# A two-layer graph kernel: layer two's own-row factors kept on chip, and one statistics instruction for two blocks' last rows

## The reference

```python
h = maximum(layernorm(x), 0)
out = h @ W_self.T + b_self                       # layer one: mean over links
agg = segment_sum(h[dst] @ W_neigh.T + b_neigh, src); count = clip(links of a node, 1)
x = x + out + agg / count
h = maximum(layernorm(x), 0)
norm = deg**-0.5 [src] * deg**-0.5 [dst]          # layer two: symmetric norm
x = x + relu(segment_sum(h[src] * norm[:, None], dst))
```

## Time and profile before

| | |
|---|---|
| median of 3 runs | 1193.75 us (1192.7 to 1194.19) |
| profiled execution, its own time | 1191.59 us |
| its span (first to last instruction) | 1189.8 us |
| VectorE, ScalarE busy | 1045.1 us, 1033.9 us |
| TensorE, GpSimd busy | 851.3 us, 783.7 us |
| mean granted TensorE clock | 0.777 of full |

### The profile page before, as it was taken

One profiled execution on the slowest core, in us unless ns is written; L12 is line 12 of the kernel. 1 busy time (PEld: TensorE's weight loads), 2 busy tenths in 40 slices (PEclk: granted clock), 3 DMA queues, 4 the chain that ended last, 5 costly groups with the idle time before them and its releaser, 6 DMA issues.

```text
span 1189.8 us, 32033 instructions
## 1 busy us (share of the span) xinstructions
PE 851.3 (72%) x10194; PEld 772.0 (65%) x10292; DVE 1045.1 (88%) x2871; ACT 1033.9 (87%) x2679; POOL 783.7 (66%) x1034
## 2 busy tenths in 40 slices
PE   1488999999999999999999952444444444444444
PEld 1378999999999999999899952343343343334343
DVE  6889999999999999999988636888888888888886
ACT  1579999999999999999989926988888988889896
POOL 3735667766767767766656127777777777777771
PEclk6699999999999999999999985555555555555555
DMA  6326666666666766666655244888888888888884
GB/s 207 117 74 182 195 203 194 203 201 193 204 191 201 208 188 203 209 189 202 195 182 180 90 183 126 281 269 274 272 259 268 280 262 266 280 262 265 273 273 185
DMA packets 76797, 252.46 MB, mean 212 GB/s; under 512 B 16114, under 2 KB 16484, under 8 KB 76676
## 3 DMA queue, kind: packets, MB, share of 16 engines
q1 hardware_dynamic: 57412, 210.46, 54.8%
q0 software_dynamic: 19264, 40.48, 13.3%
HBM read 146.50 MB, written 104.37 MB: 211 GB/s over the span
## 4 chain that ended last, share of the span: by engine, by line
PE 32%; POOL 21%; issue 19%; ACT 16%; DVE 8%; POOLq 2%; DMA 1%; SPq 0%; ACTq 0%; DVEq 0%
POOL X L663 17%; ACT work L771 12%; PE p_O L958 11%; PE p_O L946 8%; PE p_T L901 5%; PE p_T L920 4%; DVE ST L1360 3%; ACT area L787 2%; POOL work L600 2%; PE p_T L864 1%; DVE area L1419 1%; POOL factor L636 1%; PE p_O L954 1%; ACT p_T L771 1%; ACT area L795 1%
## 5 line engine op out<-in xcount | busy, mean ns | idle before, releaser
L771 ACT ACTIVATE work<-X,shift,scale 128x128 f32<-128x128 f32 x1231 | 504.0, 486 | 1.8 <-DVE shift L1394 1.8
L1360 DVE BATCH_NORM_STATS2 ST<-X 128x6 f32<-128x256 f32 x1176 | 405.8, 415 | 14.3 <-DMA X<-x_table 7.0
L663 POOL DMA_INDIRECT X<-in_x,IDX x294 | 290.1, 987 | 101.2 <-issue 70.9
L663 POOL DMA_INDIRECT X<-x_table,IDX x294 | 285.6, 971 | 92.8 <-issue 89.9
L1000 PE MATMUL p_O<-work 32*128 32x128 f32 x1600 | 156.2, 436 | 150.2 <-ACT work L771 78.5
L1000 PEld LDWEIGHTS p_O<-work 32*128 32x128 f32 x1600 | 135.3, 323 | 164.2 <-issue 116.8
L1000 PE MATMUL p_T<-work 32*128 32x128 f32 x1536 | 150.0, 436 | 125.5 <-POOL work L604 70.2
L946 PE MATMUL p_O<-wnT,area 128*128 128x128 f32 x1568 | 216.9, 282 | 8.0 <-DVE area L1419 7.8
L1000 PEld LDWEIGHTS p_T<-work 32*128 32x128 f32 x1536 | 130.0, 323 | 138.4 <-issue 118.4
L958 PEld LDWEIGHTS p_O<-wsT,area 128*128 128x128 f32 x1568 | 206.0, 192 | 7.3
L958 PE MATMUL p_O<-wsT,area 128*128 128x128 f32 x1568 | 206.6, 275 | 5.1
(11 more groups left out here) (158 smaller groups left out, 913.8 us busy)
## 6 DMA issues: line engine op xcount, KB each, us to landing
x_table<-area SPq DMA_DIRECT2D x98, 528.0 KB
X<-x_table SPq DMA_DIRECT2D x98, 528.0 KB, 4.6
X<-in_x SPq DMA_DIRECT2D x98, 512.0 KB, 4.2
out_x<-area SPq DMA_DIRECT2D x98, 512.0 KB, 5.5
X<-in_x,IDX POOLq DMA_INDIRECT x294
X<-x_table,IDX POOLq DMA_INDIRECT x294
es<-in_src SPq DMA_DIRECT2D x1, 488.5 KB, 3.6
ed<-in_dst SPq DMA_DIRECT2D x1, 488.5 KB, 4.4
```

The costliest lines, as they stand in the source:

```text
L663: nc.gpsimd.indirect_dma_start(got(s)[:, k, 0:w], None, table, bass.IndirectOffsetOnAxis(ap=IDX[:, s, k:k + 1], axis=0)).then_inc(gathered ...
L771: last = nc.scalar.activation(o, row(l, s, r), ACT.Relu, bias=shift[:, s, r:r + 1], scale=scale[:, s, r:r + 1])
L1360: last = V.bn_stats(ST[:, s, r:r + 2, :].rearrange("p r k -> p (r k)"), of)
```

## The change

A new tensor F [128, 98, 11] holds the factors of all rows and all blocks. Layer one's reciprocal of the counts goes into F[:, i, 0:8] and stays there; `rc` and its wait for `dis_ready` are gone. ScalarE's copy of the link factors goes into F[:, :, 8:11] in place of `DISL`. In layer two GpSimd multiplies only F[:, :, 8:11], in place, by the gathered rows' column D; the product for the own rows is gone, and so are the waits for `x_loaded` and `scale_made`. `scales1` reads F at the block's index. From the third block of layer two on, the statistics of the 11th rows of an even block and the odd block behind it are taken by one instruction, which interleaves the two rows, in the odd block's step.

```diff
--- before.py
+++ after.py
@@ -257,7 +257,7 @@
         work = sb("work", [P, TB * EC])
         SRC = sb("SRC", [P, DRAWS, NB + max(LOT)], i32)
         DL = sb("DL", [P, PARTS, NB])
-        DISL = sb("DISL", [P, DRAWS, NB])
+        F = sb("F", [P, NB, ROWS])
         both = sb("both", [P, 2, NB])
 
         SLOT = ROWS * XW
@@ -272,7 +272,6 @@
         sd = sb("sd", [P, max(RING), ROWS])
         rstd = sb("rstd", [P, max(RING), ROWS])
         scale = sb("scale", [P, max(RING), ROWS])
-        factor = sb("factor", [P, max(RING), ROWS])
         shift = sb("shift", [P, max(RING), ROWS])
 
         KEPT = (ROWS, DRAWS)
@@ -300,7 +299,6 @@
         verdict = sb("verdict", [1, 4, CHECKS])
         bad = sb("bad", [1, 1])
         flag = sb("flag", [1, 1], i32)
-        rc = sb("rc", [P, HT, BT])
 
         def own(l, s):
 
@@ -623,28 +621,20 @@
 
                 i, s, _ = place(1, turn, off)
                 for k in range(n):
-                    _, q, uses = place(1, turn, off + k)
-                    pool.wait_ge(x_loaded[q], (uses + len(range(q, NB, RING[0]))) * 16)
-                    pool.sem_inc(idx_seen[1], 1)
+                    _, q, _ = place(1, turn, off + k)
                     pool.wait_ge(gathered[q], landed(1, q, turn, off + k))
                     pool.sem_inc(idx_seen[1], 1)
-                if not first(i, RING[1]):
-                    pool.wait_ge(scale_made, lots(turn, off) - RING[1] // 2)
+                if first(i, 1):
+                    pool.wait_ge(s_coded, 2 * TB)
                     pool.sem_inc(idx_seen[1], 1)
-                of_own = X[:, s:s + n, 0:BT * XW].rearrange("p n (j d) -> p n j d", j=BT)[:, :, :, D]
                 of_got = X[:, s:s + n, BT * XW:ROWS * XW].rearrange("p n (k d) -> p n k d", k=DRAWS)[:, :, :, D]
-                nc.gpsimd.tensor_tensor(factor[:, s:s + n, 0:BT], of_own, of_own, ALU.mult)
-                nc.gpsimd.tensor_tensor(factor[:, s:s + n, BT:ROWS], of_got,
-                                        DISL[:, :, bass.ds(i, n)].rearrange("p k b -> p b k"), ALU.mult
+                nc.gpsimd.tensor_tensor(F[:, bass.ds(i, n), BT:ROWS], F[:, bass.ds(i, n), BT:ROWS], of_got, ALU.mult
                                         ).then_inc(factored, 1)
 
             def step(l, turn, off):
                 if l == 0 and there(l, turn, off + 1) and own_rows(off + 1):
                     last_row(turn, off + 1)
                 if l == 1 and together(turn, off + 2):
-                    if first(place(1, turn, off + 2)[0], 1):
-                        pool.wait_ge(s_coded, 2 * TB)
-                        pool.sem_inc(idx_seen[1], 1)
                     factors(turn, off + 2, together(turn, off + 2))
                 if l == 1 and there(l, turn, off + 1) and by_pool(off + 1):
                     last_row1(turn, off + 1)
@@ -726,7 +716,7 @@
                     nc.scalar.activation(codeT[:, :, :], scratch, ACT.Copy, bias=TOP, scale=-1.0).then_inc(s_coded, 1)
                 else:
                     c = slice(GROUP_BLOCKS * (m - TB), GROUP_BLOCKS * (m - TB) + GROUP_BLOCKS)
-                    nc.scalar.copy(DISL[:, :, c], scratch[:, 0:DRAWS, :]).then_inc(s_coded, 1)
+                    nc.scalar.copy(F[:, c, BT:ROWS].rearrange("p n k -> p k n"), scratch[:, 0:DRAWS, :]).then_inc(s_coded, 1)
 
             act.wait_ge(s_wT, 2)
             nc.scalar.copy(wsT[:, :], p_O[2][:, 0:D])
@@ -792,7 +782,7 @@
                 act.wait_ge(counts_read, i + 1)
                 if not first(i, HR[0]):
                     act.wait_ge(stored[0][off % HR[0]], stores_before(0, turn, off) * 16)
-                nc.scalar.activation(made(0, off % HR[0])[:, :, D], rc[:, off % HT, :], ACT.Sqrt).then_inc(dis_ready, 1)
+                nc.scalar.activation(made(0, off % HR[0])[:, :, D], F[:, i, 0:BT], ACT.Sqrt).then_inc(dis_ready, 1)
 
             def step0(turn, off):
 
@@ -1349,7 +1339,8 @@
                 if l == 1:
                     uses = uses + len(range(s, NB, RING[0]))
                 dve.wait_ge(x_loaded[s], uses * 16)
-                for r in range(0, ROWS, 2):
+                in_twos = l == 1 and not first(i, 2)
+                for r in range(0, ROWS - in_twos, 2):
                     if r == BT:
                         dve.wait_ge(gathered[s], landed(l, s, turn, off))
                     if r + 1 < ROWS:
@@ -1358,6 +1349,9 @@
                     else:
                         of = got(s)[:, r - BT, 0:D].rearrange("p (c a) -> p c a", a=1).to_broadcast([P, D, 2])
                     last = V.bn_stats(ST[:, s, r:r + 2, :].rearrange("p r k -> p (r k)"), of)
+                if in_twos and off % 2 == 1:
+                    at = (ROWS - 1) * XW
+                    last = V.bn_stats(ST[:, s - 1:s + 1, ROWS - 1, :], X[:, s - 1:s + 1, at:at + D].rearrange("p s c -> p c s"))
                 last.then_inc(st_ready[l], 1)
 
             def inverse0(turn, off):
@@ -1385,7 +1379,7 @@
                 i, s, _ = place(1, turn, off)
                 dve.wait_ge(factored, lots(turn, off))
                 dve.wait_ge(inverted[1], lots(turn, off))
-                V.tensor_tensor(scale[:, s:s + n, 0:ROWS], rstd[:, s:s + n, 0:ROWS], factor[:, s:s + n, 0:ROWS], ALU.mult
+                V.tensor_tensor(scale[:, s:s + n, 0:ROWS], rstd[:, s:s + n, 0:ROWS], F[:, bass.ds(i, n), :], ALU.mult
                                 ).then_inc(scale_made, 1)
 
             def shifts0(turn, off):
@@ -1406,7 +1400,7 @@
                 dve.wait_ge(counts_read, i + 1)
                 dve.wait_ge(n_ready[g], i + 1)
                 bank = out0(off, g)[:, :].rearrange("p (a k b) -> p a k b", a=2, k=2)
-                by = of_half(rc[:, off % HT, :].rearrange("p (a b) -> p a b", b=1).to_broadcast([P, BT, P]), g)
+                by = of_half(F[:, i, 0:BT].rearrange("p (a b) -> p a b", b=1).to_broadcast([P, BT, P]), g)
                 V.tensor_tensor(bank, bank, by, ALU.mult).then_inc(n_scaled[g], 1)
 
             def added(turn, off, g):
@@ -1423,9 +1417,7 @@
 
                 i, _, _ = place(0, turn, off)
                 dve.wait_ge(aT_sb, 2 * i + 2)
-                if not first(i, HT):
-                    dve.wait_ge(dis_ready, i - HT + 1)
-                V.reciprocal(rc[:, off % HT, :], summed(off, 1)[:, 1, 2 * P:2 * P + BT]).then_inc(counts_read, 1)
+                V.reciprocal(F[:, i, 0:BT], summed(off, 1)[:, 1, 2 * P:2 * P + BT]).then_inc(counts_read, 1)
 
             def finish1(turn, off, g):
 
```

## The result

The changed kernel takes 1185.69 us (median of four runs, 1185.0 to 1186.83) against 1193.22 us for the kernel before: the ratio is 0.9937, with a 95% interval of 0.992 to 0.9954. That is 7.5 us less, where 8.3 us less and 1185.4 us were forecast. The profiled execution took 1186.13 us around a span of 1184.3 us, which is 5.5 us less than the profiled one before, where the prediction had 8.3 us less and 1183.3 us.

What follows compares the result with a forecast made beforehand. GpSimd's queue was taken to bound layer two: 49 removed squares at 0.17 us give 8.3 us, everything else zero, so 1193.75 us goes to 1185.4 us. The range for 8 in 10 was 1182.7 to 1189.5 us.

Steps and rivals of the forecast that it cites:

- GpSimd's queue is the bound: Layer two: GpSimd waits for no engine, a pair of blocks takes 9.41 us, and up to 0.66 us can go.
- The step, not the duration, leaves the queue: GpSimd, layer two: removing L636 saves the 0.17 us to L637's start, 49 times, 8.3 us.
- The statistics save no time on VectorE: VectorE, layer two: 0.33 us less a pair only lengthens the wait for ScalarE's root, 0.66 to about 1.0 us.
- The moving address of `scale`: VectorE, layer two: reading F at the block's address costs 0 to 0.2 us behind the release, taken as nothing.
- select and L637 meet as select and L636 do now: Layer two: GpSimd's call and `scale` both move by 0.17 us, so overlap stays at most 0.15 us.
- The only place: At 728.91 us L637 took 0.68 instead of 0.21 us, just behind the start of VectorE's select L1380.
- The other loop needs 8.75 us: Layer two's tail: the loop through ScalarE and VectorE, running alone, takes 8.75 us a pair.
- The third: Layer two: VectorE's select holds L637 in every pair, 0.30 us for each of 47, 1208 us; chance 0.05.
- The first: GpSimd's queue: freed time comes back as issue or a slower L637, no change, 1193.75 us; chance 0.09.
- the second: Layer two: VectorE sets the pace and its statistics count, 16 us less, 1178 us; chance 0.04.

Runs made afterwards that it cites:

- the early select: Changed kernel with VectorE's select of the next block moved ahead of the reciprocal in layer two: 1182.14 us, ratio 0.9914 to the kernel before.
- the last variant: Changed kernel with VectorE's select ahead of the reciprocal and every second block's last row normalised by VectorE instead of GpSimd: 1149.38 us, ratio 0.9637.
- the two halves of the change: Changed kernel with the statistics as before: 1188.05 us, ratio 0.9961; kernel before with only the cross-block statistics instruction: 1190.94 us, ratio 0.9985.

## Why the prediction was right, and where it was not

- **GpSimd's queue is the bound.** Shown in three sizes: one product more is 6.8 us, one less with nothing in its way 11 us (the early select, of which about 1 us are small holds that the kernel before has too), and the last row off GpSimd as well, down to ScalarE's own work, 43.6 us. Forecast 8.3. The middle one rests on the order being worth nothing by itself, which the runs left open; the first changes nothing but GpSimd's queue.
- **The step, not the duration, leaves the queue.** L598 follows the multiply as forecast. By the traces a product is worth up to 0.19 us a pair (9.406 to 9.212 without, 9.406 to 9.594 with one more) instead of 0.17, so 8.3 to 9 us. The first of these two also has the small holds in it that the early select avoids, and by the medians one product more is 6.8 us, so the runs don't show that the term was too small.
- **The statistics save no time on VectorE.** The wait grew to 0.97 us, forecast 1.0. What the prediction lacked is that they also set when a select meets a gather, worth 0 to 2 us.
- **The moving address of `scale`: "I take nothing".** This step failed. It costs 0.13 us, within the bound of 0.2 that was given, and it was right that this doesn't lengthen GpSimd's queue directly. But "select and L637 meet as select and L636 do now" rested on it. The select came later against the multiply, its start moved from 0.64 to 0.77 us ahead of GpSimd's call in nearly every pair of the loop to 0.44 to 0.61 us ahead, and in 8 pairs the two collided. That took back 3.2 us. The address alone doesn't do this: in both kernels that have it with the statistics as before, the select starts at least 0.54 us ahead in the loop and no multiply is held, but third gathers are, by 5.5 and 5.0 us. It takes the fewer statistics too to move the loss from the gathers to the multiply, and that was not in the prediction either.
- **"The only place" of a collision.** It was not the only one in the rows. L636 at 1166.06 took 0.63 us, and a select had started at 1165.93. The prediction read only the idle time before it.
- **The other loop needs 8.75 us.** In the tail after the change ScalarE's two blocks start at 1158.22 and 1166.98, 8.76 us apart, and ScalarE alone paces the last variant at 8.48.
- **The rivals.** The third was there in its mechanism and not in its size: it was argued against with "for that to come back in each pair, the other loop must need 9.4 us", and it doesn't come back in each pair. It comes at most once in a turn of the loop, in the first of its four pairs. The first and the second are ruled out by the traces and by the two halves of the change.

That the forecast lies within 0.3 us of the median is partly luck. 3.2 us of holds were not in the sum, and 45 pairs became shorter by 5.5 us in the traces, as the profiled executions did, where the medians differ by 7.5 us; the runs of one kernel spread over about 2 us.

The collision itself could be read beforehand from the nearest row. The Trainium skill, SBUF — State Buffer, section "SBUF: two separate sides", calls the pair of ports that VectorE and GpSimd share an exclusive lock, which whoever starts first keeps for its whole instruction. The trace agrees for the multiply, which ends 0.06 us behind the select; the select, lengthened to 1.03 us while a gather was running, suggests that a gather can hold it as well, which no run here isolates. The rule doesn't tell the 8 lengthened selects from the 8 that start as late and are not.

## What to carry to other kernels

Read the limit of a stage from the engine that nobody makes wait, even if it is the least busy one, and measure the room below it in a stretch where it has nothing to do, as the tail here. An instruction's price in a full queue is the distance to the next start. When operands get addresses from a register, look at what follows the wait. Put instructions of VectorE with two SBUF operands where it waits anyway, away from GpSimd's work.

## What the runs showed of the hardware

- A multiply of GpSimd with 6 elements a partition takes 0.21 us alone and 0.61 us behind a select of VectorE (128x512, both operands in SBUF); an indirect gather whose first 0.24 us overlap such a select takes 1.05 instead of 0.95 us, and 1.42 us with 0.61 us of overlap.
- An operand addressed from a register, directly behind a wait, delays VectorE's instruction by 0.13 us (0.42 to 0.55 us behind GpSimd's call; 0.24 and 0.38 outside and inside the loop of the changed kernel).
- Chips differ. On two of them the kernel before took 1291 and 1295 us instead of 1193. Its variants moved 232 to 236 GB/s in layer two there instead of 266, and on the second of them the change made 0.1% slower what it makes 0.6% faster elsewhere.
